# Two shared-expert products of the third pair, issued before the routed experts instead of after them

## The reference

```
g = jnp.einsum('ech,ehf->ecf', buf, w_gate)
u = jnp.einsum('ech,ehf->ecf', buf, w_up)
y = jnp.einsum('ecf,efh->ech', jax.nn.silu(g) * u, w_down)
...
sh = jax.nn.silu(x @ sw_gate) * (x @ sw_up) @ sw_down
sh = jax.nn.sigmoid(x @ w_shared_gate) * sh
out = out + sh
```

## Time and profile before

| | us |
|---|---|
| median of 3 runs | 758.59 |
| lowest and highest of them | 756.6, 761.98 |
| the profiled execution's own time | 757.21 |
| its span | 755.4 |
| PE busy | 727.5 |
| DVE, ACT, POOL busy | 531.0, 464.7, 429.9 |

### The profile page before, as it was taken

One profiled execution on the slowest core, in us unless ns is written; L12 is line 12 of the kernel. 1 busy time (PEld: TensorE's weight loads), 2 busy tenths in 40 slices (PEclk: granted clock), 3 DMA queues, 4 the chain that ended last, 5 costly groups with the idle time before them and its releaser, 6 DMA issues.

```text
span 755.4 us, 12879 instructions
## 1 busy us (share of the span) xinstructions
PE 727.5 (96%) x4144; PEld 624.1 (83%) x4144; DVE 531.0 (70%) x1554; ACT 464.7 (62%) x1273; POOL 429.9 (57%) x339
## 2 busy tenths in 40 slices
PE   8799999999999999999999999999999989999996
PEld 6598889988899998889999888999877857777875
DVE  5898897689876868987686797778664225454383
ACT  5788868777986776788677678777553212222110
POOL 3545445454465588646548864655545507567356
PEclk9999999999999999999999999999999989999998
DMA  8960007600005011000401102040369889996772
GB/s 303 322 139 1 2 0 241 230 0 2 1 1 192 5 49 48 33 1 1 166 2 48 40 28 76 3 168 1 124 166 258 220 267 263 289 228 71 171 226 84
DMA packets 62418, 84.44 MB, mean 112 GB/s; under 512 B 6376, under 2 KB 50293, under 8 KB 62352
## 3 DMA queue, kind: packets, MB, share of 16 engines
q1 hardware_dynamic: 52240, 70.59, 30.4%
q0 software_dynamic: 7680, 8.95, 6.2%
q10 hardware_dynamic: 2432, 4.07, 1.5%
HBM read 54.81 MB, written 33.51 MB: 117 GB/s over the span
## 4 chain that ended last, share of the span: by engine, by line
PE 76%; DVE 12%; ACT 6%; issue 2%; DMA 2%; POOL 1%; ACTq 0%; POOLq 0%; DVEq 0%
PE PJ L1386 22%; PE OUT L1520 9%; PE U L1505 6%; PE U L1465 6%; PE U L1672 5%; PE U L1494 4%; PE U L1464 3%; PE U L1506 3%; PE U L1620 2%; PE U L1386 2%; PE XB L1691 2%; PE OUT L1691 2%; PE OUT L1620 2%; PE XB L1386 2%; ACT U L570 1%
## 5 line engine op out<-in xcount | busy, mean ns | idle before, releaser
L792 POOL TENSOR_TENSOR qsw<-qsw,sinT 128x512 f32<-128x512 f32 x95 | 125.7, 1323 | 167.4 <-ACT qsw L557 166.5
L1017 DVE CUSTOM_DVE_ANT_0 U<-U,mask 128x128 f32<-128x128 f32 (+1 forms) x256 | 86.6, 379 | 50.8 <-PE U L1465 50.4
L570 ACT ACTIVATE U<-U,nmax 128x128 f32<-128x128 f32 (+1 forms) x256 | 100.4, 392 | 32.0 <-DVE nmax L1017 31.5
L1386 PE MATMUL PJ<-hT_hi,w_hi 128*128 128x512 f32 x254 | 110.8, 436 | 1.1 <-issue 1.1
L1386 PE MATMUL PJ<-hT_lo,w_hi 128*128 128x512 f32 x254 | 100.4, 395 | 0.0
L1386 PE MATMUL PJ<-hT_hi,w_lo 128*128 128x512 f32 x254 | 100.2, 394 | 0.0
L796 POOL TENSOR_TENSOR qr<-qr,qsw 128x512 f32<-128x512 f32 x64 | 82.6, 1291 | 29.0 <-DVE qr L1001 28.4
L556 ACT ACTIVATE qsw<-PJ 64x512 f32<-64x512 f32 x96 | 57.1, 594 | 51.7 <-PE PJ L1386 42.3
L803 POOL DMA_INDIRECT slot_rows<-xn,sidx x64 | 64.8, 1012 | 40.8 <-issue 13.1
L1520 PE MATMUL OUT<-wo_hi,oT_hi 128*128 128x256 f32 x256 | 82.9, 324 | 1.4 <-DVE wo_lo L1041 1.2
L1034 DVE TENSOR_TENSOR oT_lo<-U,oT_hi 128x256 fp32r<-128x256 f32 x128 | 54.1, 423 | 37.4 <-ACT oT_hi L577 37.2
(11 more groups left out here) (227 smaller groups left out, 1837.1 us busy)
## 6 DMA issues: line engine op xcount, KB each, us to landing
wgu<-in_dram SPq DMA_DIRECT2D x32, 352.0 KB, 9.7
expert_sum<-blank SPq DMA_DIRECT2D x3, 2176.0 KB, 17.5
slot_rows<-blank SPq DMA_DIRECT2D x1, 4624.0 KB, 26.5
late_sums<-expert_sum SPq DMA_DIRECT2D x9, 512.0 KB, 8.9
wd_a<-in_dram SPq DMA_DIRECT2D x12, 352.0 KB
wraw<-in_dram SPq DMA_DIRECT2D x8, 512.0 KB, 8.7
bcm<-mod_rows SPq DMA_DIRECT2D x8, 512.0 KB, 6.8
xe<-slot_rows ACTq DMA_DIRECT2D x10, 289.0 KB, 6.7
```

Of the source, the lines that this page charges most:

```text
L570: last = act.activation(U[n % 3][:, a:z], U[n % 3][:, a:z], ACT.Exp, scale=-1.0, bias=nmax[:, n % 4, j:j + 1], accum_out=rsum[:, n % 4, j: ...
L792: pool.tensor_tensor(pair3(qsw[:, n % NQSW, :]), pair3(qsw[:, n % NQSW, :]), both(sinT[:, :]), ALU.mult).then_inc(t2_done, 1)
L1017: last = dve.tensor_tensor_reduce(out=U[n % 3][:, a:z], in0=U[n % 3][:, a:z], in1=allowed, scale=-float(HD) ** -0.5, scalar=3.4e38, op0=AL ...
L1386: last = pe.matmul(out_ap, a(c), b_(c), start=(n == 0), stop=(n == len(steps) - 1))
```

## The change

`gate_up(2, 0)` and `gate_up(2, 1)` move from behind the 35 expert steps to in front of them, and with them the SiLUs on ACT and the multiplications on DVE. The first keeps its banks PJ0 and PJ1. The second takes OUT0 for the gate and XB for the up product. The second `hidden` stands on DVE behind expert step 0. PE's waits follow: the first transposes into PJ0 wait for the first `hidden`, the first use of OUT0 and XB by the experts waits for the second. After the experts the loops over f start at 2 for pair 2.

```diff
+FAHEAD = 2
...
         def gu_banks(q, f):
             if q == 0 and f in (1, FT - 1):
                 return GU_FLUSH if f == 1 else (XB, U[2])
+            if (q, f) == (2, 1):
+                return OUT[0], XB
             return GU[f % 2]
...
             for t in range(TT):
                 shared_rows(1, t)
+            for f in range(FAHEAD):
+                silu_of(2, f)
             for n in range(E + 3):
                 expert_slot(n)
             for q in range(2, NPAIR):
-                for f in range(FT):
+                for f in range(FAHEAD if q == 2 else 0, FT):
                     silu_of(q, f)
...
             for f in range(FT):
                 hidden(1, f)
+            hidden(2, 0)
...
             for n in range(E + 3):
                 expert_slot(n)
+                if n == 0:
+                    hidden(2, 1)
             dve.wait_ge(ld_gb, 16)
-            for f in range(FT):
+            for f in range(FAHEAD, FT):
                 hidden(2, f)
...
             for t in range(TT):
                 down(1, t)
+            gate_up(2, 0)
+            pe.wait_ge(xnt_lo_done, 2 * NPAIR)
+            pe.wait_ge(pos_used, NPAIR)
+            gate_up(2, 1)
             for n in range(E + 3):
-                if n == 1:
-                    pe.wait_ge(hs_done, 2 * FT)
+                if n == 0:
+                    pe.wait_ge(hs_done, 2 * FT + 1)
+                if n == 3:
+                    pe.wait_ge(hs_done, 2 * FT + FAHEAD)
...
-                for f in range(FT):
+                for f in range(FAHEAD if q == 2 else 0, FT):
                     gate_up(q, f)
```

## The result

| | before | changed |
|---|---|---|
| median of 22 runs each, us | 756.67 | 759.76 |
| lowest, highest | 752.58, 761.98 | 755.6, 762.26 |
| profiled execution: time, span | 757.21, 755.4 | 759.68, 757.9 |

The ratio is 1.0033, 95% interval [1.0017, 1.005]: the change makes the kernel about 2.5 us slower. I had forecast 758.0 and a gain of 0.6 us. The time lies in my range and the change is within 1%, but it goes the other way. A repetition later gave 1.0039 [1.002, 1.0059] over 12 runs.

The account below looks back on a forecast made before the run. DVE's and POOL's chains, starting when the sums arrive, set the end. In front +2.05, clock gives back 2.70, so the ramp ends 0.65 earlier; taken as -0.6 at the end, median 758.59 becomes 758.0, range 754.5 to 761.

Parts of the forecast that it names:

- the products, in front: Ahead of the experts: two products end at 614.25, slot rows arrive just before 612.20, so first transposes start 2.05 us later.
- -0.65: Expert ramp on TensorE: expert 2's gate and up start at 618.22 instead of 618.87, 0.65 us earlier.
- What the clock gives back: First experts: TensorE no longer idles, full clock from the transposes on gives back 2.70 us; ramp ends 0.65 earlier.
- The products, behind: Behind the experts: the 5.60 us saved on TensorE turn into a wait of about 4.4 us for DVE before `down(2, 3)`.
- The two chains that start from the sums: End of kernel: DVE's and POOL's chains set the end, starting when the sums arrive, not when TensorE finishes pair 2.
- The sum: End of kernel: both chains move with the sums' arrival, between 0 and -0.65, taken as -0.6; 758.0 on the median.
- A: Whole kernel: TensorE decides after all; gain 5.60 + 0.65 = 6.25, 752.4 on the median; chance 0.13 including partial forms.
- B: New wait behind the experts: clock falls, end becomes slower, up to 2.7 us, about 760.6; chance 0.12.
- C: Front: experts start late and nothing comes back, clock low otherwise or second row copy late; +1.4 or more, 760.0; chance 0.08.
- D: End: DVE's gate-row multiplication gets in ahead of POOL's combining; POOL waits up to 1.1 us, 759.1; chance 0.07.

Follow-up runs that it names:

- before, repeated: The kernel before, unedited, run against itself; ratio 0.9997 [0.9972, 1.0022].
- removal only: The kernel before with ten of twelve matmuls of each of the two products left out behind the experts, nothing added in front; 1.0021, then 0.9999.
- short-lead pair: Kernel before and changed kernel, each computing one of six products of `down(1, 3)`, so TensorE is free 2.2 us earlier; 1.001 and 1.0.
- the later loads: Kernel before and changed kernel, each with SP's gate-row and residual-row loads issued behind the first slot rows; 1.005 and 1.0065.
- DVE's other order: Changed kernel with pair 2's shared-tile readings ahead of DVE's combining steps and pair 3's first multiplications between these; 1.0019.
- the busy wait: Changed kernel with 20 unread matmuls of 512 columns ahead of pair 2's last down tile, where TensorE waits for DVE; 1.0029.
- one product: Kernel before with only the first of the two products moved in front, into OUT0 and XB; 0.9972, 2.1 us faster.

## Why the prediction was wrong

**The step that failed** is "the products, in front": "I take the slot rows to arrive as now, just before 612.20". The arithmetic upon it holds: 5.45 us from the end of `down(1, 3)` to the transposes (617.50 - 612.05; forecast 5.45), and 0.9 from there to expert 0's gate and up. What failed is the other side of the comparison: a hole of 3.40 us, read from one execution, stood for every execution, so the cost in front came out as +2.05 where it is 3.3 to 3.5 with the holes of 2.16 and 1.93 us. From the start of `down(1, 0)` to the third gate and up, in us:

| profiled execution | TensorE idle in the hole | third gate and up |
|---|---|---|
| before | 3.40 | 20.55 |
| before, repeated | 1.93 | 18.09 |
| removal only, first | 1.0 | 15.81 |
| removal only, second | 2.16 | 16.98 |
| changed front, six executions | none | 20.13 to 20.16 |

Against the changed front, the four executions with the front of before differ by -0.4, +2.05, +3.2 and +4.3, 2.3 on average, where my term was -0.65. (In the stage of 28.3 us my 618.22 for the third gate and up met 618.26; of the 0.65, 0.16 came from setting it against the chain's 618.87, where the row starts at 618.71.)

That this is near the measured 2.5 is no proof of size. Followed on to the end of POOL's list, the same four differences are -1.6, +1.4, +2.1 and +2.7, 1.2 on average. The second of them, repeated before against changed, is made of +2.0 when the loads of the sums are issued, -1.4 by the instruction load and +0.9 in POOL's list, and this last is missing in some executions. So the direction has a cause that the short-lead pair supports; its size is open, and four executions account for about half of the 2.5 us.

**What the clock gives back** was mis-sized with it. I had 2.70 in every execution. From `down(1, 0)` the transposes start at 14.04 in the kernel before and at 16.08 in the changed one, 2.0 later, and the third gate and up comes 0.4 earlier: with the hole of 3.40, 2.5 us are given back. With that of 1.93 the transposes start at 12.57, 3.5 earlier than in the changed kernel, and 2.05 of it remain: 1.5 given back. With that of 2.16, where the clock did not fall, 3.3 become 3.15: 0.1.

**The products, behind.** Right. The wait was 4.39 (forecast 4.4), in the place named, and the removal alone brought nothing. The two chains that start from the sums did set the end; the end of the span kept 5.5 to 5.6 us behind POOL's in every version.

**The sum** took the arrival of the sums to follow the first result by up to its whole shift. The queue of adding DMAs passes on a part: its last issue moved by 1.45 of 2.05 us between the repeated before and the changed kernel, by 1.1 of 4.6 with the later loads. I had also taken the loads of the sums to follow that issue as before, by 3.8 to 3.9 us; in both profiles of the changed kernel and in its variants with DVE's other order and with the busy wait it is 4.3 to 4.4, in all others 3.8 to 4.0.

**A term I did not have** worked for the change: in the kernel before, one load of instructions falls into the loading of the sums, and POOL's sums come 1.4 us later (below).

**Rivals.** A is refuted. B's half clock came, but cost at most 0.9 in the traces. C had the right end, "the experts start late and nothing comes back", and near its size (+1.4 or more), with a cause that I had not thought of; I gave it 0.08. D's case came in another place: DVE's multiplication still started after POOL's first addition, but in the first profile an addition of DVE's got in ahead of it and POOL paid 0.9 us, near D's 1.1. I had asked only about the multiplication.

**The level.** Three runs of before had a median of 758.59, 22 had 756.67. My 758.0 was near the measured 759.76 partly because that first median was high: luck.

What else stays open: why the clock falls for 3.4, 6.6 or 10 us in the router's stage, and how often each occurs in the timed runs, whose traces I do not have.

## What to carry to other kernels

A hole between two engines' work is a difference of two arrival times; look in more than one execution at what sets each before filling it, and fill it with little more than its usual size. Here the holes with the usual stage were 1.0 to 2.2 us; one product (2.8 us) was worth 2 us and two (5.6 us) cost 2.5. Work taken from the busiest engine was worth nothing here, where the chain that ends the program starts from another queue, even at 96% busy.

## What the runs showed of the hardware

The queues in the 22 us from the first load of the sums, in the repeated kernel before:

```profile
q1 hardware_dynamic: 6846, 6.80, 96.2%
q8 instruction: 1, 0.02, 0.3%
```

and in the changed kernel:

```profile
q1 hardware_dynamic: 6864, 6.82, 97.7%
```

One instruction load of 0.02 MB. In the six profiled executions with it and the usual order of the sums, POOL's first sums come 17.5 to 17.8 us after the loads are issued; in the ten without it 16.1 to 16.2, once 16.8. Which kernels have it depends on how many matmuls precede that place, even if nobody reads them (twelve of 8 columns were enough). That the load is the cause is argued from this alone; no run moved it and nothing else.
